# Scores and contexts of a two-layer graph attention kernel as four 64x64 products at once, with the contexts of two graphs cut into two phases

## The reference

```
h = maximum(layernorm(x), 0)
q, k, v = h @ Wq + bq, h @ Wk + bk, h @ Wv + bv        # split into 6 heads of 64
scores = q @ k.T / sqrt(64)                            # per graph and head, 128 x 128
probs = softmax(where(adj, scores, scores - 9e15))
x = x + (probs @ v, heads joined) @ Wf + bf
```

## Time and profile before

| | us |
|---|---|
| Median of 3 runs (1850.74 to 1851.70) | 1851.24 |
| The profiled execution, its own time | 1853.11 |
| Its span, first to last instruction | 1851.3 |
| PE busy | 1821.8 (98%) |
| DVE, ACT, POOL busy | 1621.9, 1561.2, 1490.9 |

### The profile page before, as it was taken

The page is one execution under the profiler, slowest core; times in us unless marked ns, Lnnn a source line. Parts: engine busy times, 40 slices in busy tenths (PEclk is TensorE's granted clock), DMA queues, the critical chain, the costliest instruction groups (busy, mean ns, idle before and its releaser), DMA issues.

```text
span 1851.3 us, 54324 instructions
## 1 busy us (share of the span) xinstructions
PE 1821.8 (98%) x17210; PEld 1050.4 (57%) x17210; DVE 1621.9 (88%) x5551; ACT 1561.2 (84%) x4793; POOL 1490.9 (81%) x1781
## 2 busy tenths in 40 slices
PE   7899999999999999999999999999999999999998
PEld 3455555555555555555555555555555555555555
DVE  7889898898988988889888888988889888898876
ACT  5888888888888888888888888888888888888884
POOL 4678888888888888888888888888888888888761
PEclk8999999999999999999999999999999999999999
DMA  6656666666666666666667666667666666666655
GB/s 195 175 171 185 204 205 193 197 205 199 208 197 199 200 193 209 205 197 194 193 207 203 203 196 200 201 199 215 195 196 194 198 207 197 200 179 193 194 169 180
DMA packets 439942, 363.32 MB, mean 196 GB/s; under 512 B 207700, under 2 KB 406888, under 8 KB 439656
## 3 DMA queue, kind: packets, MB, share of 16 engines
q1 hardware_dynamic: 439656, 359.86, 65.1%
HBM read 184.30 MB, written 175.37 MB: 194 GB/s over the span
## 4 chain that ended last, share of the span: by engine, by line
PE 86%; DVE 4%; DMA 3%; SPq 3%; issue 2%; ACT 1%; POOL 1%; DVEq 0%; ACTq 0%; POOLq 0%
PE ps_qk L683 12%; PE ps_shared L683 12%; PE ps_shared L685 12%; PE ps_shared L684 12%; PE ps_qk L684 12%; PE ps_qk L685 12%; PE ps_shared L780 7%; PE ps_scores L800 7%; SPq L375 2%; DMA p_dram<-p_blocks 1%; DVE probs L1316 1%; DMA p_moved<-p_dram 1%; DVE qk_lo L1296 1%; POOL probs L551 1%; ACT probs L1013 1%
## 5 line engine op out<-in xcount | busy, mean ns | idle before, releaser
L1013 ACT ACTIVATE probs<-probs,row_min 128x128 f32<-128x128 f32 x1512 | 583.1, 391 | 2.5 <-DVE row_rcp L1281 1.5
L551 POOL TENSOR_TENSOR probs<-probs,row_rcp 128x768 f32<-128x768 f32 x252 | 370.2, 1469 | 215.5 <-DVE row_rcp L1281 215.2
L1316 DVE CUSTOM_DVE_ANT_0 probs<-ps_scores,mask,minus_scale 128x128 f32<-128x128 f32 x1512 | 429.6, 347 | 0.9 <-issue 0.6
L568 POOL TENSOR_TENSOR p_half<-p_moved,p_half 128x768 f16<-128x768 f32 x236 | 388.0, 1644 | 1.6 <-ACT p_half L988 1.6
L1296 DVE SCALAR_TENSOR_TENSOR qk_lo<-ps_qk,qk_bias,qk_hi 128x512 f16<-128x512 f32 x384 | 278.7, 747 | 77.2 <-ACT qk_hi L996 76.1
L1013 ACT ACTIVATION_READ_ACCUMULATOR probs<-probs,row_min 128x1 f32 x1512 | 288.8, 191 | 0.0
L996 ACT ACTIVATE qk_hi<-ps_qk,qk_bias 128x512 f16<-128x512 f32 x384 | 258.1, 672 | 14.6 <-PE ps_qk L685 14.6
L547 POOL TENSOR_TENSOR x_tile<-x_tile,out_bias 128x384 f32<-128x384 f32 x256 | 257.7, 1007 | 1.1 <-DVE out_bias L1240 1.1
L1327 DVE SCALAR_TENSOR_TENSOR x_tile<-ps_shared,out_scale,x_tile 128x384 f32<-128x384 f32 x256 | 157.1, 613 | 111.2 <-PE ps_shared L685 108.6
L683 PE MATMUL ps_shared<-wf_hi,ct_hi 128*128 128x384 f16 x768 | 250.6, 326 | 2.4 <-DVE ct_lo L1290 2.4
L685 PE MATMUL ps_shared<-wf_hi,ct_lo 128*128 128x384 f16 x768 | 250.8, 327 | 0.0
(11 more groups left out here) (152 smaller groups left out, 3997.7 us busy)
## 6 DMA issues: line engine op xcount, KB each, us to landing
p_dram<-p_blocks SPq DMA_DIRECT2D x256, 384.0 KB, 2.4
p_moved<-p_dram SPq DMA_DIRECT2D x1008, 96.0 KB, 2.4
h_dram<-h_blocks SPq DMA_DIRECT2D x252, 192.0 KB, 2.6
h_moved<-h_dram SPq DMA_DIRECT2D x1008, 48.0 KB, 2.0
x_tile<-in_x SPq DMA_DIRECT2D x128, 192.0 KB, 2.9
out_x<-x_tile SPq DMA_DIRECT2D x128, 192.0 KB, 2.7
adj_u<-in_adj SPq DMA_DIRECT2D x64, 64.0 KB, 2.6
p_half<-p_dram SPq DMA_DIRECT2D x16, 96.0 KB, 2.3
```

The costliest lines, as they stand in the source:

```text
L551: nc.gpsimd.tensor_tensor(probs_of(t, i), probs_of(t, i), row_rcp[i % 2][:, :].rearrange("p (a o) -> p a o", o=1) .to_broadcast([P, HEADS, ...
L568: nc.gpsimd.tensor_tensor(p_part(i, 1), p_moved[i % 2][:, :, :].rearrange("p a n -> p (a n)"), p_part(i, 0), ALU.subtract).then_inc(p_set, 1)
L1013: ins = nc.scalar.activation(tile[:, s, :], tile[:, s, :], ACT.Exp, bias=row_min[i % 2][:, s:s + 1], scale=-1.0, accum_out=row_sum[i % 2][ ...
L1316: ins = nc.vector.tensor_tensor_reduce(tile[:, s, :], score_bank(i, s // PAIRS)[:, (s % PAIRS) * P:(s % PAIRS + 1) * P], mask[b][:, i, :], ...
```

## The change

Nothing changes but PE's program and one new semaphore, ctx_begun.

**Scores.** Each product is cut into two halves of 64 queries. A group is now four products of 64 rows x 64 stationary columns and 128 moving columns, one in each quarter of the array: 36 products per graph instead of 18, 9 groups as before.

**Contexts.** Where both graphs of a pair use split probabilities (117 pair blocks in slots 3 to 61), their contexts are computed together. The 128 keys are cut into two halves of 64. In phase 0 the first graph takes its keys 0 to 63 and the second its keys 64 to 127, in phase 1 the other way round, so that the two graphs always write from different row halves into different banks. A phase has 9 groups of four products (36), two graphs x two heads. Both graphs' waits (contexts_free, twice) stand before phase 0. The counter ctx_summed is raised for both graphs at the end of phase 1. Phase 1 waits for ctx_begun, which phase 0 raises.

**Order.** A pair block was score, score, contexts, contexts. It is now score(t, i), phase 0, score(t, i+1), phase 1. In the few blocks of slots 1 to 3 whose probabilities are not split, and in last_units, the contexts stay as they were; all scores use quarters.

```diff
+            def contexts_free(t, i):
+                vu, vi = graph_at(t, i, 8)
+                if i % 2 and vu < B:
+                    pe.wait_ge(v_set, unit_count(vu, PER, vi + 1))
+                else:
+                    wait(pe, out_added, unit_count(t, PER, i - 1))
+                    pe.wait_ge(v_set, unit_count(t, PER, i + 1))
+                pe.wait_ge(p_set, halved_count(t, i))
+            def half_contexts(graphs, phase):
+                if phase == 1:
+                    pe.wait_ge(ctx_begun, halved_count(*graphs[1]) - 1)
+                for c in range(PAIRS):
+                    for k, (a, b) in enumerate(((0, 0), (1, 0), (0, 1))):
+                        for g, (t, i) in enumerate(graphs):
+                            keys = slice(((g + phase) % 2) * DH, ((g + phase) % 2 + 1) * DH)
...
+                            for odd in range(2):
+                                hd = 2 * c + odd
+                                last = c == PAIRS - 1 and k == 2
+                                mm = pe.matmul(ctx_bank(i)[odd * DH:(odd + 1) * DH, c * P:(c + 1) * P],
+                                               v_part(t, i, a)[keys, hd * DH:(hd + 1) * DH],
+                                               turned[keys, odd * PAIRS + c, :, :],
+                                               start=phase == 0 and c == 0 and k == 0, stop=phase == 1 and last)
+                            if last:
+                                mm.then_inc(ctx_summed if phase else ctx_begun, 1)
...
                         for odd in range(2):
                             rows = slice(odd * DH, (odd + 1) * DH)
-                            mm = pe.matmul(score_bank(i, odd)[:, c * P:(c + 1) * P], q[b][rows, c, cols],
-                                           k[b][rows, KT + c, cols], start=first, stop=last)
+                            for half in range(2):
+                                part = slice(half * DH, (half + 1) * DH)
+                                mm = pe.matmul(score_bank(i, odd)[part, c * P:(c + 1) * P],
+                                               q[b][rows, c, i * NODES + half * DH:i * NODES + (half + 1) * DH],
+                                               k[b][rows, KT + c, cols], start=first, stop=last)
...
             def slot(t):
                 for i in range(PER):
                     ou, oi = graph_at(t, i, -5)
-                    if exists(t) and i % 2 == 0:
+                    pair = [(pu, pi) for pu, pi in pair_at(t, i) if exists(pu)]
+                    if len(pair) == 2 and halved(pair[0][0]) and halved(pair[1][0]):
                         score(t, i)
+                        contexts_free(*pair[0])
+                        contexts_free(*pair[1])
+                        half_contexts(pair, 0)
                         score(t, i + 1)
-                    for pu, pi in pair_at(t, i):
-                        if exists(pu):
+                        half_contexts(pair, 1)
+                    else:
...
                             apply_probs(pu, pi)
```

More of the change, by code:

```diff
@@ L257, in build @@
         p_set = sem("p_set")
+        ctx_begun = sem("ctx_begun")
         ctx_summed = sem("ctx_summed")
@@ L755, in project_qk @@
                     mm.then_inc(qk_projected, 1)
+            def contexts_free(t, i):
[13 more added lines that the diff above has]
+                            keys = slice(((g + phase) % 2) * DH, ((g + phase) % 2 + 1) * DH)
+                            turned = p_part(i, b).rearrange("p (a s k) -> p s a k", a=QUADS, s=HEADS)
+                            for odd in range(2):
[7 more added lines that the diff above has]
+                                mm.then_inc(ctx_summed if phase else ctx_begun, 1)
             def apply_probs(t, i):
@@ L820, in slot @@
                     ou, oi = graph_at(t, i, -5)
-                    if exists(t) and i % 2 == 0:
+                    pair = [(pu, pi) for pu, pi in pair_at(t, i) if exists(pu)]
+                    if len(pair) == 2 and halved(pair[0][0]) and halved(pair[1][0]):
                         score(t, i)
+                        contexts_free(*pair[0])
+                        contexts_free(*pair[1])
+                        half_contexts(pair, 0)
                         score(t, i + 1)
-                    for pu, pi in pair_at(t, i):
-                        if exists(pu):
+                        half_contexts(pair, 1)
+                    else:
+                        if i % 2 == 0:
+                            score(t, i)
+                            score(t, i + 1)
+                        for pu, pi in pair:
                             apply_probs(pu, pi)
```

## The result

The changed kernel took **1917.03 us** (median of 4 runs, 1916.01 to 1922.64) against 1850.99 (4 runs, 1848.52 to 1851.70): a ratio of 1.0367, with a 95% interval of 1.0355 to 1.0379. It is 66 us slower where 30 were forecast, and 1917 lies above the upper end of the range, 1912. The direction was right, the size was not.

The account below looks back on a forecast made before the run. PE, busy 98% of the span, was taken as the bound. New wait 0.34 less saved shape change 0.09 gave +0.25 us a block, +29.3 over 117 blocks; with +1 for irregularity, 1881 us from 1851, range 1868 to 1912.

Parts of the forecast that it names:

- The pace of a group of four: PE's scores and split contexts: four quarter products take 0.056 us a group, the same as two products before.
- Rival (A): PE's scores and contexts: four products don't run at the pace of two; 2086 us in full, 1912 halfway; 14%.
- The common start time of two products: Score groups in the earlier timeline: a group's two products are sent much closer together than 0.028 us.
- The overhead of some 60 cycles for each matmul: Counter-argument at PE's products: as every product's pace, a group of four takes 0.10 us, some 190 us slower overall.
- The saved change of shape: Between scores and contexts of a block: both now have one shape, saving 0.09 us a block.
- The place and the time of the add: Ahead of phase 0: the residual add ends 0.79 us after block start; PE stands 0.34 us.
- Rival (B): Ahead of phase 0: the moved wait is already fulfilled when PE arrives, so the kernel gets faster, 1841 us; 7%.
- From the add's end to PE's next load the one such wait shows 0.06 us: Restart ahead of phase 0: PE's load follows the add by 0.06 us, so phase 0 can't begin before 0.85 us.
- Some 70 more pieces hidden behind 1850 us cost nothing: Fetching PE's added instructions: 1.1 us a piece, taken as no cost; 76 us if PE sat out each in full.
- The +1 us for irregularity: Irregular blocks: late adds, 3.7 us in all, set against shrinking PE stops of 7.4 us; 1 us added.
- Rival (C): Block banks: ACT's and DVE's half microsecond isn't caught up, PE meets late banks; 0.1 us a block, 1893 us; 6%.
- +0.34 of wait: Ahead of phase 0: PE's new wait for the residual add behind only one score, 0.34 us a block.

Follow-up runs that it names:

- both_behind: split6 with the order score, score, phase 0, phase 1, so both scores stand ahead of the contexts in quarters; 1893.33 us, ratio 1.0244 against the kernel before.
- moved_wait: The kernel before, products and order unchanged, with the five waits of both graphs' contexts also put between the two scores; 1907.71 us, ratio 1.0317.
- add_last: The changed kernel with its five waits ahead of phase 0 merged into three, and out_added carried by the weight load; 1901.19 us, ratio 1.0295 against the kernel before.
- counted_late: The kernel before, with ctx_summed of a pair's first graph raised only together with the second's; 1849.44 us, ratio 1.0004.
- fetch_more: The kernel before, with three always fulfilled waits put ahead of every projection product, 8,528 more instructions; 1866.65 us, ratio 1.0092.
- split6: add_last with six of the second score's nine groups ahead of phase 0 and three behind it; 1895.65 us, ratio 1.0252 against the kernel before.

## Why the prediction was right in sign and wrong in size

**The pace of a group of four: right.** 0.056 us, in the scores (16 steps in 0.89 us) and in phase 0 (0.50 us for nine groups). Rival (A), given 14%, falls. The common start time of two products, which the prediction read in the earlier trace rows, is only the start of the merged row; in the records the two start 3 ns apart, so the conclusion from it was right. The overhead of some 60 cycles for each matmul, which the prediction quoted from the Trainium skill, "TensorEngine Tiling (Array Packing)", section "Instruction Overhead", is not the pace of products in different parts of the array: four of them pass in 0.056 us, where the prediction's estimate from that page was 0.10.

**The saved change of shape: right.** 0.08 us in both_behind, 0.09 forecast.

**The place and the time of the add: right.** It ends 0.79 us after the block's start, and PE stands there in nearly every block. moved_wait puts the whole of this wait, as written, at 59 us. Rival (B), that the moved wait is fulfilled in time, falls. The profile puts that stop down to "issue" (44.8 us, 113 times, about 0.40 each) and not to the add, as the prediction said; that is so because the sequencer held the wait. add_last names the add.

**"From the add's end to PE's next load the one such wait shows 0.06 us": this step failed first.** The row was read rightly, but there the load carried the wait itself. With out_added among several waits that the sequencer takes one after another, it is 0.21 us, in after and in moved_wait. 0.15 × 117 = 17.6 us; add_last, with three waits and out_added on the load, has 0.06 again and gave back 13 to 16.

**"Some 70 more pieces hidden behind 1850 us cost nothing": this step failed second, and its error is up to 24 us.** The page's row gave 1.1 us a piece and 0.5% of the DMA time, and I set what PE would have to sit out at nothing, without a row that showed it. In after PE stood for 7.3 us in eight stops that I read as this. And I did not ask whom else a piece holds up. SP's issues take 1.01 us instead of 0.41 where they coincide with one, and SP's transfers are on the way from DVE's transposes to ACT, which the profile of before showed already: ACT waited 24.5 us for p_moved, 43 times. With the instructions that fill them, 34 pieces cost 17 us in before and 33 cost 22 in after. The pieces are the one cause of irregularity in after that a run has raised by itself.

**The +1 us for irregularity** set the growing lateness against PE's longer stop and let them cancel. In moved_wait they do. In after they don't, as the pieces come with the quarters. Rival (C) had the place right (late banks) and a size half as large (12 us), but its cause, the late count, cost nothing in counted_late, which is the kernel before with that count.

**The sum with measured terms:** the regular block +0.34 of wait, +0.15 of restart, −0.09 of shape is 0.40 us, × 117 = 47; irregular blocks 24; together 71 us against 69.5 between the profiled executions.

**What stays open.** How much of add_last's gain is the smaller number of waits, and how much the one that the load carries, is not separated. Why an issue of SP that meets a piece is longer (which resource the two share) is shown by no run; more pieces could not be had without more instructions on PE, so that fetch_more varies both. That the issues lengthen where pieces coincide, in the trace of every run, and that PE's regular pace is unchanged in fetch_more, speak for the pieces. Of the 27.5 us in after's irregular distances 7.3 are PE's stops with nothing to wait for, and 8.5 are waits ahead of phase 0 that last longer than the usual one; how the rest divides between the pieces, the 0.1 us less between blocks than in moved_wait, and the contexts that come late for both graphs is not separated either; a moved_wait with the late count was not run.

## What to carry to other kernels

Before you move a wait, ask not only when the other engine is done but which instruction will carry the wait: carried by the load itself it cost 0.06 us, as one of several in front of it 0.21, at every pass. And more instructions on an engine are not free because the engine keeps its pace: look at whose work becomes longer while they are fetched, whether that one has slack, and whether the engine stands anywhere with nothing to wait for. A stop on the busiest engine is also the others' slack; taking it away gives back less than its length (19 us by the median block in split6, 6 to 8 gained).

## What the runs showed of the hardware that I had not expected

- Four products of 64 rows x 64 columns in the four quarters take 0.056 us together, as two products that fill the array do.
- An instruction piece of 16 KB (2.24 MB in 137) is 1.1 to 1.2 us on its way, and an SP DMA issue that coincides with one takes 1.01 us instead of 0.41.
- With contexts in phases, at 0.014 us a product, PE stood eight times in after, three of them in phase 1 and five in the projections, with nothing to wait for, up to 2.13 us, and each time went on 1.30 to 1.53 us after a piece had landed.
- One fulfilled wait instruction more ahead of each projection product (0.16 to 0.22 us) costs no pace; with two the distance between blocks goes from 14.02 to 17.80 us.
